# Masks of a row-sorting network: from bytes in SBUF to words in PSUM, with the step's instructions in another order

## The reference, cut to what matters

```python
xh = x[:, :ch]                       # half of the channels: sort by columns, then by rows
...
q = conv1x1(x, w_qkv)
cat = concat(dwconv3(q), dwconv5(q), dwconv7(q))
qkv = conv1x1(cat, w_fuse) + b_fuse
q1, k1, q2, k2, v = split(qkv, 5)
vf = v.reshape(b, c, hw)             # hw = 3136
idx = argsort(vf)                    # sort each row of v ...
vs = take(vf, idx)
gat = lambda t: take(t.reshape(b, c, hw), idx)   # ... and carry q1, k1, q2, k2 along
out1 = reshape_attn(gat(q1), gat(k1), vs, temp, True)
out2 = reshape_attn(gat(q2), gat(k2), vs, temp, False)
inv = argsort(idx)                   # undo the sort on the product
out = conv1x1(take(out1, inv) * take(out2, inv), w_proj)
```

## Time and profile before

| what | value |
|---|---|
| median of three runs | 17148.6 us |
| the profiled execution | 17148.49 us |
| its span | 17146.6 us |
| VectorE busy | 16016.6 us, 93% |
| ScalarE busy | 7247.1 us, 42% |
| TensorE busy | 6760.6 us, 39% |
| the eight sorts | from 3334 to about 14210 us |

### The profile page before, as it was taken

One profiled execution on the slowest core, in us unless ns is written; L12 is line 12 of the kernel. 1 busy time (PEld: TensorE's weight loads), 2 busy tenths in 40 slices (PEclk: granted clock), 3 DMA queues, 4 the chain that ended last, 5 costly groups with the idle time before them and its releaser, 6 DMA issues.

```text
span 17146.6 us, 106420 instructions
## 1 busy us (share of the span) xinstructions
PE 6760.6 (39%) x40644; PEld 2812.9 (16%) x40644; DVE 16016.6 (93%) x10433; ACT 7247.1 (42%) x5055; POOL 0.2 (0%) x4
## 2 busy tenths in 40 slices
PE   6888855570025614613722632642561101210010
PEld 4444431120011111201211211211111000000000
DVE  6999988899999999999999999999999998879978
ACT  0000003343453453444444444345345337868854
POOL 0000000000000000000000000000000000000000
PEclk9999987785567757856866866875775555555555
DMA  0000012110001000000100100100100001131232
GB/s 18 13 25 17 21 37 71 54 31 11 10 10 31 23 10 26 27 10 22 31 10 10 40 15 10 35 19 10 31 23 10 25 14 41 52 86 51 71 73 65
DMA packets 297993, 509.96 MB, mean 30 GB/s; under 512 B 54685, under 2 KB 258685, under 8 KB 287413
## 3 DMA queue, kind: packets, MB, share of 16 engines
q1 hardware_dynamic: 297460, 502.90, 10.3%
HBM read 298.39 MB, written 204.33 MB: 29 GB/s over the span
## 4 chain that ended last, share of the span: by engine, by line
DVE 60%; issue 10%; ACT 6%; PE 3%; DMA 1%; SPq 1%; DVEq 0%; ACTq 0%
DVE arena L1070 21%; DVE arena L1077 15%; DVE arena L1054 5%; DVE masks L1046 5%; DVE arena L1061 5%; DVE arena L1550 3%; PE psum L1332 2%; ACT arena L1497 2%; DVE arena L1548 2%; ACT arena L1020 2%; DVE arena L1401 1%; ACT arena L1507 1%; DMA masks<-row_masks 1%; ACT arena L1010 1%; DVE arena L1407 1%
## 5 line engine op out<-in xcount | busy, mean ns | idle before, releaser
L1020 ACT ACTIVATE arena<-arena 128x4096 f32<-128x4096 f32 (+26 forms) x1456 | 3072.3, 2127 | 5883.2 <-DVE arena L1077 5883.0
L951 PE MATMUL psum<-arena,wt 128*32 128x448 f32 x31360 | 3379.9, 594 | 1873.0 <-ACT arena L967 1126.7
L1070 DVE COPY_PREDICATED arena<-masks,arena 128x4096 f32<-128x4096 uint8 (+26 forms) x1456 | 4017.3, 2787 | 9.3 <-ACT arena L1020 9.3
L1077 DVE COPY_PREDICATED arena<-masks,arena 128x4096 f32<-128x4096 uint8 (+26 forms) x1456 | 4001.3, 2775 | 0.6
L951 PEld LDWEIGHTS psum<-arena,wt 128*32 128x32 f32 x31360 | 1047.2, 119 | 4208.2 <-issue 2660.3
L1287 PE MATMUL psum<-ident,arena 128*112 128x128 f32 x896 | 194.4, 386 | 3557.8 <-ACT arena L1208 2826.6
L1550 DVE COPY_PREDICATED arena<-arena 128x2048 f32<-128x2048 uint8 (+28 forms) x364 | 972.2, 2687 | 241.8 <-ACT arena L1507 241.6
L1046 DVE TENSOR_TENSOR masks<-arena 128x1568 uint8<-128x1568 f32 (+21 forms) x912 | 1033.9, 1192 | 128.9 <-ACT arena L1010 128.9
L731 PE MATMUL psum<-arena 128*128 128x392 f32 x3072 | 1053.8, 496 | 31.9 <-DVE arena L633 31.8
L1054 DVE TENSOR_TENSOR arena<-arena 128x1568 f32<-128x1568 f32 (+21 forms) x912 | 1056.3, 1220 | 0.0
L1061 DVE TENSOR_TENSOR arena<-arena 128x1568 f32<-128x1568 f32 (+21 forms) x912 | 1037.6, 1197 | 0.3
(11 more groups left out here) (126 smaller groups left out, 6794.2 us busy)
## 6 DMA issues: line engine op xcount, KB each, us to landing
arena<-xpad SPq DMA_DIRECT2D x896, 108.5 KB, 2.4
xpad<-arena SPq DMA_DIRECT2D x8, 1924.0 KB, 7.0
arena<-in_x SPq DMA_DIRECT2D x8, 1568.0 KB, 10.4
x3d<-arena SPq DMA_DIRECT2D x8, 1568.0 KB, 5.2
prodd<-arena SPq DMA_DIRECT2D x8, 1568.0 KB, 5.2
arena<-prodd SPq DMA_DIRECT2D x8, 1568.0 KB, 13.8
arena<-x3d SPq DMA_DIRECT2D x8, 1568.0 KB, 10.1
out<-arena SPq DMA_DIRECT2D x64, 196.0 KB, 4.5
```

The source lines that it names most:

```text
L951: last = nc.tensor.matmul(psum[C * b:C * b + C, n % C_BANKS, 0:CROWS * W], wt[:, g, C * w:C * w + C], cx[i % 2][b][:, y0:y0 + CROWS, x0:x0 ...
L1020: last = nc.scalar.activation(packed_view(ptmp, here, piece, NP), pair_views(pay[b], piece, NP)[0], ACT.Copy)
L1070: last = nc.vector.copy_predicated(lo, wide_mask(q, piece, at), hi)
L1077: last = nc.vector.copy_predicated(hi, wide_mask(q, piece, at), packed_view(ptmp, here, piece, NP))
```

## The change

- The mask lies in PSUM banks 4 to 7, one float word a pair (`pmask`), written by `compare`. The masked copies read it there as 32-bit words, four times each. There is one mask buffer for VectorE, no longer four.
- ScalarE copies each mask from PSUM to bytes in SBUF (`mask_copy`, 624 copies in all), from where SP stores it as before. The first `lower` of a step waits for that copy (`d_mcp`) in place of waiting for `compare`.
- On VectorE a step is now comparison, min, max, and the four masked copies. The comparison waits for the last masked copies of the step before (`d_hi`).
- On ScalarE a step is mask copy, `keep_v` and `keep_pay` of the next step, and the four slots. `keep_v` is issued one step later than before.
- The attention's weights are transposed in banks 0 and 1, in turn with keys and queries (`tr`, `trc` count them all), and its products lie in banks 2 and 3. `bits` is not called.

```diff
@@ -976,6 +976,21 @@
+        pmask = psum[:, 4:8, :].rearrange("p k n -> p (k n)")
+        d_mcp = sem("d_mcp")
+        d_sems.append(d_mcp)
+
+        def mask_copy(act, q):
+
+            act.wait_ge(d_mk, q + 1)
+            if q >= 4:
+                act.wait_ge(d_mst[q % 4], 16 * (q // 4))
+            n = ROW_NET[q][2]
+            nc.scalar.activation(masks[:, q % 4, 0:n], pmask[:, 0:n], ACT.Copy).then_inc(d_mcp, 1)
+
+        def bits(at, piece):
+            return packed_view(pmask.bitcast(mybir.dt.uint32), at, piece, 1)
+
         def lot_rows(q, k):
@@ -985,12 +1000,12 @@
             n = size(piece)
-            return masks[:, q % 4, at:at + n].unsqueeze(2).to_broadcast([P, n, NP])
+            return pmask.bitcast(mybir.dt.uint32)[:, at:at + n].unsqueeze(2).to_broadcast([P, n, NP])
...
             for q, (at, _, n) in enumerate(ROW_NET):
-                sp.wait_ge(d_mk, q + 1)
+                sp.wait_ge(d_mcp, q + 1)
                 sp.dma_start(row_masks[t, :, at:at + n], masks[:, q % 4, 0:n]).then_inc(d_mst[q % 4], 16)
@@ -1024,13 +1039,12 @@
             keep_pay(0, 1)
-            keep_v(1)
             for s in range(SR):
+                mask_copy(act, s)
                 if s + 1 < SR:
+                    keep_v(s + 1)
                     keep_pay(s + 1, 0)
                     keep_pay(s + 1, 1)
-                if s + 2 < SR:
-                    keep_v(s + 2)
                 for _ in range(SLOTS):
@@ -1040,10 +1054,11 @@
                 dve.wait_ge(d_vcp, q + 1)
-                if q >= 4:
-                    dve.wait_ge(d_mst[q % 4], 16 * (q // 4))
+                if q:
+                    dve.wait_ge(d_hi[0], q)
+                    dve.wait_ge(d_hi[1], q)
                 for piece, at in ROW_NET[q][1]:
-                    last = nc.vector.tensor_tensor(packed_view(masks[:, q % 4, :], at, piece, 1),
+                    last = nc.vector.tensor_tensor(packed_view(pmask, at, piece, 1),
                                                    packed_view(vtmp, at, piece, 1), pair_views(vrow[b], piece, 1)[1],
@@ -1064,7 +1079,7 @@
                 if k == 0:
-                    dve.wait_ge(d_mk, q + 1)
+                    dve.wait_ge(d_mcp, q + 1)
                 for piece, at, _ in lot_rows(q, k):
@@ -1077,32 +1092,25 @@
-            compare(0)
-            lower_v(0)
-            upper_v(0)
             for s in range(SR):
-                ahead = s + 1 < SR
+                compare(s)
+                lower_v(s)
+                upper_v(s)
+                next(beside, None)
                 lower(s, 0)
                 next(beside, None)
-                if ahead:
-                    compare(s + 1)
                 upper(s, 0)
...
                 next(beside, None)
-                if ahead:
-                    lower_v(s + 1)
                 upper(s, 1)
-                if ahead:
-                    upper_v(s + 1)
-                next(beside, None)
             for _ in beside:
...
         E_LAST = E_NEXT + E_OUT + 12
-        E_NAMES = ("ssq", "rt", "rn", "sc", "tr", "trc", "a", "am", "ex", "p", "pt", "ptc", "o", "oc", "st", "ch")
+        E_NAMES = ("ssq", "rt", "rn", "sc", "tr", "trc", "a", "am", "ex", "p", "o", "oc", "st", "ch")
         es = {n: sem("e_" + n) for n in E_NAMES}
@@ -1115,7 +1123,8 @@
         Q_GROUPS = [(0, 1, 2, 3), (4, 5, 6)]
-        TRS = len(K_GROUPS) + NF * len(Q_GROUPS)
+        TRS = len(K_GROUPS) + NF * len(Q_GROUPS) + NF
+        Q_AT, P_AT = (7, 9, 11, 14), (13, 16, 17, 18)
@@ -1161,7 +1170,7 @@
             def queries(a, f, g):
-                n = TRS * a + len(K_GROUPS) + 2 * f + g
+                n = TRS * a + Q_AT[f] + g
                 act.wait_ge(e["tr"], n + 1)
@@ -1171,13 +1180,13 @@
             def weights(a, f):
-                n = NF * a + f
-                act.wait_ge(e["pt"], n + 1)
+                n = TRS * a + P_AT[f]
+                act.wait_ge(e["tr"], n + 1)
                 if a and f == 0:
...
                 nc.scalar.activation(ept[:, 4 * f:4 * f + 4, :],
-                                     psum[:, 4 + n % 2, :].rearrange("p (a m) -> p a m", m=P),
-                                     ACT.Copy).then_inc(e["ptc"], 1)
+                                     psum[:, n % 2, :].rearrange("p (a m) -> p a m", m=P),
+                                     ACT.Copy).then_inc(e["trc"], 1)
@@ -1198,7 +1207,7 @@
                         nc.scalar.activation(out1_segment(b, True, n // 2)[:, 392 * (n % 2):392 * (n % 2) + 392],
-                                             psum[:, 6 + n % 2, 0:392], ACT.Copy).then_inc(e["oc"], 1)
+                                             psum[:, 2 + n % 2, 0:392], ACT.Copy).then_inc(e["oc"], 1)
                 for n in range(2 * NF):
@@ -1253,7 +1262,7 @@
                     if n >= 2:
-                        dve.wait_ge(e["pt"], n - 1)
+                        dve.wait_ge(e["tr"], TRS * ((n - 2) // NF) + P_AT[(n - 2) % NF] + 1)
                     w3 = w.rearrange("p (a m) -> p a m", m=P)
@@ -1269,7 +1278,7 @@
                 f, h = n // 2, n % 2
-                nc.vector.tensor_tensor(segment(eo, False, f)[:, 392 * h:392 * h + 392], psum[:, 6 + n % 2, 0:392],
+                nc.vector.tensor_tensor(segment(eo, False, f)[:, 392 * h:392 * h + 392], psum[:, 2 + n % 2, 0:392],
                                         out1_segment(b, False, f)[:, 392 * h:392 * h + 392],
@@ -1295,7 +1304,7 @@
                     n = NF * a + f
-                    pe.wait_ge(e["trc"], TRS * a + len(K_GROUPS) + 2 * (f + 1))
+                    pe.wait_ge(e["trc"], TRS * a + Q_AT[f] + 2)
                     if n >= 2:
@@ -1317,19 +1326,21 @@
                     pe.wait_ge(e["p"], n + 1)
-                    if n >= 2:
-                        pe.wait_ge(e["ptc"], n - 1)
+                    m = count[0]
+                    assert m == TRS * a + P_AT[f]
+                    pe.wait_ge(e["trc"], m - 1)
                     for g in range(NF):
-                        last = nc.tensor.transpose(psum[:, 4 + n % 2, P * g:P * g + P],
+                        last = nc.tensor.transpose(psum[:, m % 2, P * g:P * g + P],
                                                    eam[n % 2][:, P * g:P * g + P], ident[:, :])
-                    last.then_inc(e["pt"], 1)
-                pe.wait_ge(e["ptc"], NF * (a + 1))
+                    last.then_inc(e["tr"], 1)
+                    count[0] += 1
+                pe.wait_ge(e["trc"], TRS * (a + 1))
                 for n in range(8):
...
                     for g in range(NF):
-                        last = nc.tensor.matmul(psum[:, 6 + n % 2, 0:392], ept[:, 4 * f + g, :],
+                        last = nc.tensor.matmul(psum[:, 2 + n % 2, 0:392], ept[:, 4 * f + g, :],
                                                 segment(vrow[b], a == 0, g)[:, 392 * h:392 * h + 392],
```

## The result

After the change the kernel takes **18009.94 us** (median of 4 runs, 18008.69 to 18012.71), before it 17147.13 (4 runs of the same chip, 17145.42 to 17150.89). The ratio is 1.0503, with a 95% interval of 1.0485 to 1.0521: 863 us slower. The forecast was 17,880, +732.

The account below looks back on a forecast made before the run. VectorE was taken to bound the kernel. 324 + 476 + 60 - 68 - 60 = +732 us on about 17,148 gave 17,880 us, 4.3% slower; own range 17,650 to 18,100, 80% range 17,320 to 18,260.

Parts of the forecast that it names:

- What bounds the kernel: VectorE, busy 93% of the span: a microsecond it works or waits longer inside a sort is one of the result.
- The wait for the mask copy: First masked copy of a step waits for ScalarE's mask copy behind four slots: +476 us, plus +60 in the last level.
- Squarings and scalings: Four slots of attention work ahead of the mask copy, eight such steps a sort: VectorE waits 5.2 us each, 42 us.
- Products: Two steps a sort with four attention products each ahead of the mask copy: some 8 us of wait each, 16.
- the last level of the six sorts: Ten steps with up to 4220 words in the second lot: about 1 us of wait each, +60 us over six sorts.
- Order on VectorE: Four waits a step on the instruction right ahead, 0.13 us each over 624 steps, not hidden: +324 us.
- The comparison's wait on L1010: Comparison's wait at the ends of the sorts goes away: 8.5 us in each of eight sorts, -68 us.
- The masked copies themselves: 2912 masked copies gain a third of 184 us from less company in SBUF, a PSUM operand being free: -60 us.
- The rest at nothing: Comparison's output to PSUM, mask stores, the attention's banks and ScalarE's mask copies where not counted elsewhere: no cost.
- B: Rival: the mask stream was the brake; masked copies fall to 4.41 us per 4096 words, -565, total 17,375; chance 0.13.
- C: Rival: word masks let masked copies move more than one word per cycle, -3,718, total 14,320, faster; chance 0.17.
- D: Rival: a PSUM mask makes each masked copy dearer, +380 us, total 18,260; chance 0.10.

Follow-up runs that it names:

- the first run: The kernel before with only the attention's PSUM banks of the change, masks and order as before: 17143.98 us, ratio 1.000.
- the version that beats both: The kernel before, with ScalarE issuing `keep_v` ahead of the second lot's carry copy in a sort's last level: 17066.8 us, ratio 0.9955.

## Why the prediction was right, and where its sum was off

Held against 863 us measured, the sum of 732 is 131 short. Step by step:

- **What bounds the kernel**: right. The idle time that a run took from VectorE inside the sorts came off the result: 506 less 10 that came up in the attention slots for 497 with the mask copy ahead of the slots, 64 for 61 with the comparison's waits exchanged.
- **The wait for the mask copy**, 476 + 60 = 536: measured 528.3 less the 9.3 of the earlier trace rows = 519. Right in size, and in mechanism by the run that moved the copy ahead of the slots. Squarings and scalings were put at 5.2 a block and are 4.7, because the prediction worked out a step of 1568 pairs for all of them. For that size it was close (wait 4.91, mask copy 1.46 against the estimated 1.5); at 784 pairs carry copy and mask copy are shorter (1.11 and 0.81) and the wait is 3.92. Products were put at 8 in each of two steps, 16 a sort, and are 16.5. By place, the first 40 steps of the seven sorts hold 462 (forecast 476) and the last level of the six sorts some 41 (forecast 60). Another 15, four waits in the last sort behind copies on ScalarE that prepare the undoing (L1463), were in no term, so that the total fits better than its parts.
- **Order on VectorE**, 324: this is the term that was mis-sized. Step "4 x 624 x 0.13" took four equal dependences. With the comparison's brought down to 0.034 by the exchanged waits, the kernel stands 17451.65 - 17143.09 = 309 above the one before. Back on comes the comparison's wait that is gone, 69; off go the mask wait, 24 in place of 9, and 12 more of waits in the attention slots (128.2 against 116.2): some 350, or 0.14 for each dependence. The two traces give the same without this remainder: VectorE's instructions in the sorts take 263 us longer from start to start (10923.4 against 10660.2), most of it lost overlap, and the gaps of 0.034 make 84. On top, the comparison as the change writes it costs 61 more, since it has three waits and carries the wrong one. 350 + 61 = 411, 87 above the sum. The first sort, with only 3.2 us of waits for the mask copy, shows this term nearly alone: it is 45 longer, where 30 to 40 were expected.
- **The comparison's wait on L1010**, -68: right, 128.9 to 59.6, -69.
- **The masked copies themselves**, -60: wrong, no gain shows, rather a loss of 6 us from start to start (7817.4 against 7811.4). The step took the 2.3% between the copies of the sort and those of the undoing as company in SBUF, of which a third would go with the mask stream. In the new order with byte masks the copies are as fast as with word masks out of PSUM: 4735 and 4741 ns for the first copy of 4096 words with byte and word masks. What the 2.3% are was not tried; taking the mask out of SBUF made no copy faster:

```profile
L1086 DVE COPY_PREDICATED arena<-masks,arena 128x4096 f32<-128x4096 uint8 x104 | 492.5, 4735 | 0.0
```
```profile
L1086 DVE COPY_PREDICATED arena<-psum,arena 128x4096 f32<-128x4096 uint32 x104 | 493.1, 4741 | 12.2 <-ACT masks L989 12.2
```

- **The rest at nothing** (banks, comparison's output, stores): right; the banks by the first run, the comparison at 1007.5 us after against 1002.9 with bytes.

The terms as measured: 411 + 519 - 69 + 0 = +861.

The rivals fall by the same rows. B wanted every copy at 4.41 and C under 4; measured were 4724 and 4671 ns in the kernel after, inside the 4.6 to 4.8 that the forecast named. (B's -565 was also worked out too small: 4.41 is 7.5% under 4.77, and 7.5% of 8018.6 is 605.) D wanted +380 for masks in PSUM; between the kernels with byte and with word masks in the new order the masked copies differ by 6. The Trainium skill, "VectorE: DVE Perf Modes", section on the TRN2 errata, gives 58 cycles out of SBUF and 120 out of PSUM; an estimate from that is 65 ns more for each of the 2912 copies whose mask lies in PSUM, 188 us between those two runs; the trace, with its 6 us, does not agree.

## What to carry to other kernels

An independent instruction between two dependent ones on the same engine is worth its place: it hid 0.14 us for each pair here, some 350 us in all, and the gain looked for in return (cheaper masks) was not there. Before paying for an operand's move, run the other half of the change alone: one kernel with the new order and the old masks gives the price of the order, and what is left is the masks. A copy that the critical engine waits for goes ahead of the filler work on its engine's list, not behind it; and among several waits of an instruction, the one that is fulfilled last is written first.

## What the runs showed that I had not expected

- An instruction of the engines carries one wait in all records here; the others become an instruction of their own in front of it. If that one holds the wait that is fulfilled last, the gap between the two instructions of VectorE is 0.104 us with one wait in it, 0.133 with two, 0.202 with two such instructions; if it holds waits already fulfilled it costs nothing (0.034, as for a single wait).
- A wait on the instruction right ahead costs 0.14 us here, although it is fulfilled when that ends: 0.034 of gap, and an overlap of some 0.10 lost. The Trainium skill, "VectorE: DVE Perf Modes", section "The DRAIN you can't avoid", says that a semaphore after each of a chain of copies costs nothing extra. The kernels here differ from that: some 350 us for 4 x 624 waits. With no run that leaves a wait out between dependent instructions, whether it is the wait or the dependence that costs stays open.
- Recorded durations depend on more than the instruction. The masked copies lost 140 us of recorded time with byte masks and the new order (8018.6 to 7879.0), while from start to start they grew by 207 (7604.0 to 7811.4). Even with the same order on VectorE the recorded sum is 7981.5 with the attention in four banks and 8089.5 in the version that beats both, where from start to start it is 7605.3 and 7597.1. In the kernel before neighbouring records overlap by 0.10 to 0.15 us at the median of each kind of pair, and by 0.25 to 0.42 and more in a tenth of the pairs, so busy sums of two kernels must not be set against each other; from start to start they can.
- Why masked copies of the same 4096 words take 4.41 us at some places and 4.7 on the mean was not tried and stays open.
